# A fused transformer block: in its attention, the value product goes to the end of the next unit, and turned blocks go by DRAM

## The chip, the cores and the metric

The kernel is one program on one core of a Trainium2 chip. The time is the device time of one execution in microseconds; of the kernel before three executions were timed, and one more was profiled. TensorE is called PE, VectorE DVE, ScalarE ACT, GpSimd POOL and SyncE SP.

## The reference, cut to what matters

Four residual steps on x of shape (4, 512, 512). The change is in the third, an attention with 16 heads of width 128 whose keys and values come from `ctx_2048`.

```python
def _L1_xattn_ref(inputs_q, inputs_kv, Wq, Wk, Wv, Wo):
    q = (inputs_q @ Wq).reshape(b, sq, H, HD) * (1.0 / np.sqrt(HD))
    k = (inputs_kv @ Wk).reshape(b, skv, H, HD)
    v = (inputs_kv @ Wv).reshape(b, skv, H, HD)
    scores = jnp.einsum('bqhd,bkhd->bhqk', q, k)
    attn = jax.nn.softmax(scores, axis=-1)
    ctx = jnp.einsum('bhqk,bkhd->bqhd', attn, v).reshape(b, sq, H * HD)
    return ctx @ Wo

x = x + _L0_xattn_ref(_layernorm(x, axis=-1), ctx_2048, mask_Bx1xS2_ff0)
x = x + _L0_ffn_ref(_layernorm(x, axis=-1), ...)
x = x + _L1_xattn_ref(_layernorm(x, axis=-1), ctx_2048, L1_xattn_Wq, L1_xattn_Wk, L1_xattn_Wv, L1_xattn_Wo)
x = x + _L1_ffn_ref(_layernorm(x, axis=-1), L1_ffn_W1, L1_ffn_W2, L1_ffn_W3)
```

## The kernel before

Each step is a phase with a block of its own for each engine, and the engines meet at a barrier between phases. Every product of the attention is made from float32 numbers that are split into a high and a low part (`_hi`, `_lo`), in three matmuls: high by high, high by low, low by high (`three_pass`, line 46). ACT copies the high part out of the PSUM bank, DVE subtracts it from the bank to get the low part. POOL splits the weights and the turned probabilities, which lie in SBUF.

`attention_phase` (line 1109) works in 64 units. A unit is one head of one batch. Batches come in two pairs (`r`), a pair has 32 units in 8 groups (`g`) of four (`p` = 0 to 3): p = 0 and 2 are batch 0 of the pair, p = 1 and 3 batch 1, and each group covers two heads. The first and last group of a pair stand in the program by themselves, those between are a loop.

In unit n PE does: the scores of unit n (12 matmuls of 512 columns into four score banks), the queries of unit n+1 (12, into `qk_bank`), `weigh`, the product of the values with the turned probabilities of unit n-1 (12, into `vo_bank`), the keys of unit n+1 (12, again into `qk_bank`, so only when the low part of the queries is out), and the output projection of unit n-1 (12 matmuls in four tiles through two banks). Values of a whole group (four times 24 matmuls of 256 columns, `project_v`, also into `vo_bank`) stand between output tiles: two in p = 0, one in p = 1, one in p = 3.

The probabilities take the longest way. DVE takes the maxima (line 1417), ACT the exponentials (1330), DVE turns 32x32 blocks (1408) into `blocks`, then a reciprocal (1424) signals `p_movable`. SP then issues 16 transfers of 64 KB, SBUF to SBUF, that put the blocks in place (`move`, 1192 to 1197); they fill `pT_raw` in four quarters. For each quarter ACT makes the high part (`turned`, 1321) and POOL the low part (`low`, 1255), and only then `weigh` may run. ACT does its four quarters at the end of its unit.

Between the pairs lies the layer norm of batches 2 and 3. DVE takes its row statistics in one piece behind unit 1 (`stats.compute`, lines 94 to 126), and those of the last phase's batches 0 and 1 behind unit 33. In unit 31 PE turns the normalised rows through the score banks (`tensor_turn`, 187), ACT and DVE copy them out (195, 202).

Each engine works its own list in order; semaphores order the lists against each other. There is no scheduler: the order is that of the code.

## Time and profile before

| | |
|---|---|
| median of three runs | 2359.31 us (2358.37 to 2359.66) |
| the profiled execution | 2352.57 us, of which the span is 2350.9 us |
| attention, first scores to last output | 605 to 1790 us of the span |
| granted PE clock, mean of the span | 0.95 |
| PE busy over the span | 1977.7 us (84%) |

The profiled execution is one run; its own time is 6.7 us under the median. The span counts from the first to the last instruction. A row's "idle before" is the time in which its engine stood still ahead of it, with the work whose end released it. Matmuls are pipelined, so a row's duration (0.39 us) is longer than the distance to the next start; the distance is what a matmul costs.

### The profile page before, as it was taken

How to read it: one execution, taken by the hardware profiler on the slowest of the kernel's cores; microseconds unless marked ns; L12 is line 12 of the kernel's file. 1: busy time of each engine (PE TensorE's matmuls, PEld its weight loads, DVE VectorE, ACT ScalarE, POOL GpSimd, SP SyncE). 2: the span in 40 equal slices, each digit the busy share in tenths (PEclk: the TensorE clock that was granted, in tenths of full speed). 3: DMA queues.
4: the chain of work that ended last, by engine and by line, in shares of the span. 5: the costliest groups of instructions: out<-in, count | busy, mean ns of one | idle time of the engine just before them, and what ended most of it. 6: DMA issues, size and time to landing. Idle time of an engine off the chain costs nothing. (4 is left out here: it accounts for less than half of the span.)

```text
span 2350.9 us, 29076 instructions
## 1 busy us (share of the span) xinstructions
PE 1977.7 (84%) x9625; PEld 1618.6 (69%) x9625; DVE 1350.1 (57%) x2075; ACT 830.9 (35%) x1603; POOL 1047.1 (45%) x857
## 2 busy tenths in 40 slices
PE   0259858880879999999887999999996999999999
PEld 0127647660757787777776788787775788888887
DVE  7883558776565655656557566556565533333333
ACT  3212158770434444444433344444442211111111
POOL 2655532216555655656645665565645101222200
PEclk9779979995889999999988999999998999999999
DMA  4053399985223333333322332333322000000001
GB/s 163 0 211 99 122 321 383 381 300 166 81 71 95 85 87 92 85 96 92 103 73 76 91 96 77 92 100 83 85 70 90 25 12 28 27 27 27 0 1 72
DMA packets 138772, 245.90 MB, mean 105 GB/s; under 512 B 23872, under 2 KB 49216, under 8 KB 138688
## 3 DMA queue, kind: packets, MB, share of 16 engines
q1 hardware_dynamic: 121280, 186.11, 25.4%
q0 software_dynamic: 17408, 58.73, 8.7%
q8 instruction: 46, 0.75, 0.1%
q14 instruction: 38, 0.31, 0.0%
HBM read 136.22 MB, written 41.42 MB: 76 GB/s over the span
## 5 line engine op out<-in xcount | busy, mean ns | idle before, releaser
L1255 POOL TENSOR_TENSOR t_pT_lo<-t_pT_raw,t_pT_hi 128x512 fp32r<-128x512 f32 x256 | 329.1, 1291 | 380.7 <-ACT t_pT_hi L1321 374.5
L1321 ACT ACTIVATE t_pT_hi<-t_pT_raw 128x512 fp32r<-128x512 f32 x256 | 161.0, 630 | 296.5 <-DMA t_pT_raw<-t_blocks 296.4
L1408 DVE STREAM_TRANSPOSE t_blocks<-t_probs 128x512 f32<-128x512 f32 x256 | 172.0, 701 | 70.1 <-ACT t_probs L1330 68.9
L1714 DVE TENSOR_TENSOR f_lin<-f_lin,f_silu 128x512 f32<-128x512 f32 x64 | 44.6, 699 | 287.0 <-PE f_lin L51 287.0
L1330 ACT ACTIVATE t_probs<-t_score,t_sums 128x512 f32<-128x512 f32 x256 | 173.0, 681 | 87.1 <-DVE t_sums L1417 49.3
L1400 DVE SCALAR_TENSOR_TENSOR x_res<-t_out,t_sums,x_res 128x512 f32<-128x512 f32 x256 | 180.0, 743 | 10.3 <-PE t_out L51 10.3
L1641 POOL TENSOR_TENSOR f_w_hi<-w_raw,f_zeros 128x1024 fp32r<-128x1024 f32 x16 | 30.5, 1904 | 317.6 <-PE f_gate L51 314.3
L1417 DVE TENSOR_REDUCE t_sums<-t_score 128x1 f32<-128x512 f32 x256 | 162.4, 683 | 0.0
L51 PE MATMUL t_vo<-t_wv_hi,t_cT_hi 128*128 128x256 f32 x512 | 146.3, 286 | 1.8 <-DVE t_v_lo L1387 1.4
L1674 ACT ACTIVATE f_silu<-f_gate 128x512 f32<-128x512 f32 x64 | 38.3, 598 | 307.1 <-PE f_gate L51 307.1
L51 PE MATMUL t_vo<-t_wv_hi,t_cT_lo 128*128 128x256 f32 x512 | 144.8, 283 | 0.0
L51 PE MATMUL t_vo<-t_wv_lo,t_cT_hi 128*128 128x256 f32 x512 | 144.8, 283 | 0.0
L51 PE MATMUL t_qk<-t_cT_hi,t_wk_hi 128*128 128x512 f32 x256 | 105.2, 411 | 36.0 <-DVE t_q_lo L1378 35.8
L1383 DVE TENSOR_TENSOR t_k_lo<-t_qk,t_k_hi 128x512 fp32r<-128x512 f32 x64 | 44.2, 691 | 154.2 <-ACT t_k_hi L1304 154.2
L1387 DVE TENSOR_TENSOR t_v_lo<-t_vo,t_v_hi 128x512 fp32r<-128x512 f32 x64 | 44.2, 691 | 153.1 <-ACT t_v_hi L1310 153.1
L51 PE MATMUL t_vo<-t_pT_hi,t_v_hi 128*128 128x512 f32 x256 | 103.5, 404 | 29.0 <-POOL t_pT_lo L1255 29.0
L51 PE MATMUL t_qk<-t_xT_hi,t_wq_hi 128*128 128x512 f32 x256 | 101.7, 397 | 18.5 <-DVE t_xT_lo L202 18.5
L51 PE MATMUL t_out<-t_wo_hi,t_o_hi 128*128 128x512 f32 x256 | 102.0, 399 | 16.1 <-DVE x_res L1400 13.1
L1734 DVE TENSOR_TENSOR x_res<-f_down,x_res 128x512 f32<-128x512 f32 x128 | 87.9, 688 | 42.9 <-PE f_down L51 42.8
L51 PE MATMUL f_gate<-f_xT_hi,f_w_hi 128*128 128x512 f32 x256 | 101.0, 395 | 8.4 <-POOL f_w_lo L1644 5.3
L51 PEld LDWEIGHTS t_vo<-t_wv_hi,t_cT_hi 128*128 128x128 f32 x512 | 97.9, 191 | 10.3 <-DVE t_v_lo L1387 8.4
L51 PE MATMUL t_qk<-t_cT_lo,t_wk_hi 128*128 128x512 f32 x256 | 102.2, 399 | 0.0
...
## 6 DMA issues: line engine op xcount, KB each, us to landing
t_pT_raw<-t_blocks SPq DMA_DIRECT2D x1024, 64.0 KB, 2.0
e_up_raw<-in_L_ffn_Wrt_up_dram SPq DMA_DIRECT2D x47, 512.0 KB, 6.7
e_down_raw<-in_L_ffn_Wrt_down_dram SPq DMA_DIRECT2D x47, 512.0 KB, 6.3
...
e_xg<-tokens_by_expert SPq DMA_DIRECT2D x47, 256.0 KB, 6.5
outputs_by_expert<-e_y_out SPq DMA_DIRECT2D x47, 256.0 KB, 6.7
wq_raw<-in_L_xattn_Wq_dram POOLq DMA_DIRECT2D x32, 256.0 KB, 3.7
wk_raw<-in_L_xattn_Wk_dram POOLq DMA_DIRECT2D x32, 256.0 KB, 3.4
```

The costliest lines, as they stand in the source:

```text
L51: ins = pe.matmul(out, w(k), x(k), start=(k == 0 and j == 0), stop=(k == k_tiles - 1 and j == 2))
L1255: pool.tensor_tensor(pT_lo[:, q], pT_raw[:, q], f32(pT_hi[:, q]), ALU.subtract).then_inc(p_ready, 1)
L1321: act.activation(pT_hi[:, q], pT_raw[:, q], ACT.Copy).then_inc(p_hi_ready, 1)
L1330: act.activation(probs[:, t % 2, :], score_bank[t][:, :], ACT.Exp, bias=neg_max[:, t:t + 1], accum_out=total[:, t:t + 1]).then_inc(exp_rea ...
L1383: dve.tensor_tensor(k_lo[:, :], qk_bank[:, :], f32(k_hi[:, :]), ALU.subtract).then_inc(k_ready, 1)
L1387: dve.tensor_tensor(v_lo[:, b, 2 * half:2 * half + 2, :], vo_bank[:, :].rearrange("p (t d) -> p t d", t=2), f32(v_hi[:, b, 2 * half:2 * ha ...
L1400: dve.scalar_tensor_tensor(out=x_tile, in0=out_bank[t % 2][:, :], scalar=inv[:, b, t:t + 1], in1=x_tile, op0=ALU.mult, op1=ALU.add).then_i ...
L1408: dve.transpose(blocks[:, :, :, t, :].rearrange("p a t j -> p t a j"), probs[:, t % 2, :].rearrange("p (t a j) -> p t a j", a=Q4, j=BLK)). ...
L1417: dve.tensor_reduce(neg_max[:, t:t + 1], score_bank[t][:, :], AX.X, ALU.max, negate=True).then_inc(max_ready, 1)
L1674: act.activation(silu[:, k, :], gate_bank[k][:, :], ACT.Silu).then_inc(silu_ready, 1)
L1714: dve.tensor_tensor(lin_bank[k][:, :], lin_bank[k][:, :], silu[:, k, :], ALU.mult).then_inc(mid_done, 1)
L1734: dve.tensor_tensor(x_tile, down_bank[t][:, :], x_tile, ALU.add).then_inc(added, 1)
```

## The change

PE's order within a unit is new. Unit n now has: scores of n, queries of n+1, one piece of values (p = 0 to 2; it goes into score bank 1 once unit n's second exponential has read it), output tiles 0 and 1 of unit n-2, keys of n+1 (into score bank 0), output tiles 2 and 3 of n-2, and last `weigh` of unit n-1. In p = 3 the piece of values stands behind `weigh` and goes into score bank 3. Queries and head outputs have a bank of their own (`q_bank`, `o_bank`). The output of a unit is thus two units behind its scores, and four sums are kept instead of two.

On SP a unit issues 8 transfers of 256 KB: four from `blocks` to a DRAM buffer, each from 32 partitions, and four back from DRAM to 128 partitions of `pT_raw`. ACT handles the quarters of unit n-1 between the exponentials of unit n. DVE takes the row statistics in three pieces behind different units, and the layer norm's turning is spread over units 30 and 31.

```diff
-        sums = al.sb("sums", [4, TB])
-        neg_max, total, inv = sums[:, 0], sums[:, 1], sums[:, 2:4]
+        sums = al.sb("sums", [6, TB])
+        zeros, neg_max, inv = sums[:, 0], sums[:, 1], sums[:, 2:6]
-        qk_bank = al.ps("qk", [S])
-        vo_bank = al.ps("vo", [S])
+        q_bank = al.ps("q", [S])
+        o_bank = al.ps("o", [S])
...
-            def move(n):
-                sp.wait_ge(p_movable, n + 1)
+            def move(n, p):
                 for q in range(Q4):
-                    for a in range(Q4):
-                        dst = pT_raw[a * BLK:(a + 1) * BLK, q].rearrange("p t n -> p (t n)")
-                        src = blocks[q * BLK:(q + 1) * BLK, a].rearrange("p t u j -> p (t u j)")
-                        sp.dma_start(dst, src).then_inc(p_moved[q], 16)
+                    if q == 0:
+                        sp.wait_ge(p_movable, n + 1)
+                    elif not (known(n) and n == 0):
+                        sp.wait_ge(p_ready, (n - 1) * Q4 + (q + 1))
+                    sp.dma_start(moved[p % 2, q].rearrange("a i n -> i a n"),
+                                 blocks[q * BLK:(q + 1) * BLK].rearrange("p a t u j -> p a (t u j)")).then_inc(p_out[q], 16)
+                for q in range(Q4):
+                    sp.wait_ge(p_out[q], 16 * (n + 1))
+                    sp.dma_start(pT_raw[:, q].rearrange("p t n -> p (t n)"),
+                                 moved[p % 2, q].rearrange("a i n -> (a i) n")).then_inc(p_moved[q], 16)
...
             def group(r, g):
+                n, h1, h2 = 4 * g, 2 * g + 1, 2 * g + 2
+                boundary = known(g) and g == GROUPS - 1
+                final = known(g) and g == PAIRS * GROUPS - 1
+                if not (known(g) and g == 0):
+                    low(r, n - 1, after=("o", h1 - 2))
                 split(r, "q", h1, q_done, 2 * h1)
                 split(r, "k", h1, k_done, 2 * h1, after=("q", h1))
+                low(r, n, after=("k", h1))
+                split(r, "o", h1 - 1, out_done, 2 * TB * (h1 - 1))
+                low(r, n + 1, after=("o", h1 - 1))
+                if not final:
+                    split(r, "q", h2, q_done, 2 * h2)
+                    split(r, "k", h2, k_done, 2 * h2, after=("q", h2))
+                if boundary:
+                    ctx_lo(1, 0)
+                    ctx_lo(1, 1)
+                low(r, n + 2, after=None if final else ("k", h2))
+                if not final:
                     split(r, "v", g + 1, v_done, 4 * g + 4)
+                if boundary:
+                    ctx_lo(1, 2)
+                    ctx_lo(1, 3)
+                split(r, "o", h1, out_done, 2 * TB * h1, after=None if final else ("v", g + 1))
...
             def unit(r, g, p):
                 n = 4 * g + p
+                last = known(n) and n == LAST
+                if not (known(n) and n < 2):
+                    head_output(n - 2)
+                if p == 0:
+                    values(4 * g, 0, 0, score_bank[3])
                 for t in range(TB):
                     act.wait_ge(max_ready, n * TB + (t + 1))
+                    if not (known(n) and n == 0 and t < 2):
                         act.wait_ge(p_turned, n * TB + (t - 1))
                     act.activation(probs[:, t % 2, :], score_bank[t][:, :], ACT.Exp, bias=neg_max[:, t:t + 1],
+                                   accum_out=inv[:, p, t:t + 1]).then_inc(exp_ready, 1)
+                    if t == 3 and not last:
+                        query(n + 1)
+                    if not (known(n) and n == 0):
+                        turned(n - 1, t)
+                if p < 3:
+                    values(4 * g + 1 + p, (0, 1, 1)[p], (1, 0, 1)[p], score_bank[1])
                 if not last:
                     key(n + 1)
+                if known(n) and n in (UNITS - 2, UNITS - 1):
+                    i = n - (UNITS - 2)
+                    for c in (2 * i, 2 * i + 1):
+                        ctx_hi(1, c)
+                    ln.scalar_hi(act, 2 + i, xT_hi, i)
...
-                        dve.wait_ge(p_moved[q], 64 * n)
+                        dve.wait_ge(p_out[q], 16 * n)
...
             def unit(r, g, p):
                 n = 4 * g + p
+                last = known(n) and n == LAST
+                outputs = not (known(n) and n < 2)
+                before = r - 1 if p < 2 and known(g) and g == GROUPS else r
                 for t in range(TB):
                     dve.wait_ge(scored, n * TB + (t + 1))
                     dve.tensor_reduce(neg_max[:, t:t + 1], score_bank[t][:, :], AX.X, ALU.max,
                                       negate=True).then_inc(max_ready, 1)
+                    if p == 0 and t == 0:
+                        values(4 * g, 0, 0, score_bank[3])
+                turn(n, 0)
+                turn(n, 1)
+                if outputs:
+                    head_output(n - 2)
+                turn(n, 2)
+                turn(n, 3)
                 if not last:
                     project_q(n + 1)
+                dve.wait_ge(p_turned, (n + 1) * TB)
+                if not (known(n) and n == 0):
+                    dve.wait_ge(p_ready, (n - 1) * Q4 + 1)
+                dve.reciprocal(inv[:, p, :], inv[:, p, :]).then_inc(p_movable, 1)
+                if p < 3:
+                    values(4 * g + 1 + p, (0, 1, 1)[p], (1, 0, 1)[p], score_bank[1])
+                for t in range(2):
+                    if outputs:
+                        add(before, n - 2, (p - 2) % 4, t)
                 if not last:
                     project_k(n + 1)
                 for t in range(2, TB):
+                    if outputs:
+                        add(before, n - 2, (p - 2) % 4, t)
+                if known(n) and n in (UNITS - 2, UNITS - 1):
+                    i = n - (UNITS - 2)
+                    ln.vector_lo(dve, 2 + i, xT_hi, xT_lo, i)
+                    if i == 0:
+                        ln.vector_norm(dve, 3, 3)
 
             def group(r, g):
                 for p in range(4):
                     unit(r, g, p)
+                    if known(g) and g == 0:
+                        if p < 2:
+                            stats.read(dve, 2 + p)
+                        elif p == 2:
+                            stats.finish(dve, 2, 2)
+                        else:
+                            ln.vector_norm(dve, 2, 2)
+                    if known(g) and g == GROUPS:
+                        if 0 < p < 3:
+                            stats.read(dve, p - 1)
+                        elif p == 3:
+                            stats.finish(dve, 0, 2)
...
+                if not (known(n) and n == 0):
+                    pe.wait_ge(exp_ready, (n - 1) * TB + 1)
+                project("k", score_bank[0], b, cT_hi, cT_lo, k_done)
...
+                outputs = not (known(n) and n < 2)
+                if known(n) and n in (UNITS - 1, UNITS):
+                    pe.wait_ge(ln.lo_ready, (n - UNITS + 4) * TB)
                 pe.wait_ge(q_ready, n + 1)
                 pe.wait_ge(k_ready, n + 1)
                 for t in range(TB):
                     if not first:
                         pe.wait_ge(exp_ready, (n - 1) * TB + (t + 1))
+                        if t == 1:
+                            pe.wait_ge(v_ready, 4 * g + (0, 2, 3, 4)[p])
+                    if t == 3 and p == 0:
+                        pe.wait_ge(v_ready, 4 * g + 1)
                     three_pass(pe, score_bank[t][:, :], lambda k: q_hi[:, t * P:(t + 1) * P],
                                lambda k: q_lo[:, t * P:(t + 1) * P], lambda k: k_hi[:, :], lambda k: k_lo[:, :],
                                1).then_inc(scored, 1)
                 if not last:
                     project_q(n + 1, 1 - b, 2 * g + (p + 1) // 2 + 1)
+                if p < 3:
+                    project_v(n, (0, 1, 1)[p], (1, 0, 1)[p], 1)
+                if outputs:
+                    output(n - 2, b, 2 * g + p // 2, (0, 1))
+                if known(n) and n in (UNITS - 1, UNITS):
+                    pe.wait_ge(c_ready, 6 + 2 * (n - UNITS + 1))
                 if not last:
                     project_k(n + 1, 1 - b, 2 * g + (p + 1) // 2 + 1)
+                if outputs:
+                    output(n - 2, b, 2 * g + p // 2, (2, 3))
+                if known(n) and n in (UNITS - 2, UNITS - 1):
+                    pe.wait_ge(k_ready, n + 2)
+                    pe.wait_ge(v_ready, 4 * g + 4)
+                    ln.tensor_turn(pe, 2 + n - (UNITS - 2), bank_free=lambda t: pe.wait_ge(exp_ready, n * TB + (t + 1)))
                 if not first:
+                    weigh(n - 1, 1 - b, (1, 0, 0, 1)[p], 4 * g + (0, 2, 4, 4)[p])
+                if known(n) and n == UNITS - 1:
+                    pe.wait_ge(ln.lo_ready, 4 * TB)
+                if p == 3 and not last:
                     pe.wait_ge(w_ready["v"], g + 2)
+                    project_v(n, 0, 0, 3)
...
+            ln.tensor_turn(pe, 1, bank_free=lambda t: pe.wait_ge(ln.lo_ready, t + 1))
             pe.wait_ge(c_ready, 2)
+            pe.wait_ge(ln.lo_ready, TB + 1)
...
+            output(LAST - 1, 0, PAIRS * H, range(TB))
             weigh(LAST, 1, 1, 2 * PAIRS * H)
             output(LAST, 1, PAIRS * H, range(TB))
```

Of the lists of POOL, ACT, DVE and PE the diff shows the lines that stand there now; the old ones are in the kernel above. Bank names in the helpers are left out.

Three places in the lists of the engines. Semaphores that an earlier phase has freed show under that phase's name: `a_added` is here the semaphore of the maxima, `a_amax_ready` and `a_amax_over` those of queries and keys, `a_scale_ready` that of the values.

On ACT, unit 2 (p = 2), before:

```order
L1330 ACTIVATE t_probs,t_sums<-t_score,t_sums 128x512 [waits t_p_turned,a_added] x4
L1300 ACTIVATE t_q_hi<-t_qk 128x512 [waits a_amax_ready]
L1315 ACTIVATE t_o_hi<-t_vo 128x4x4x32 [waits t_o_done]
L1304 ACTIVATE t_k_hi<-t_qk 128x512 [waits a_amax_over]
L1321 ACTIVATE t_pT_hi<-t_pT_raw 128x512 [waits t_p_moved0]
L1321 ACTIVATE t_pT_hi<-t_pT_raw 128x512 [waits t_p_moved1]
L1321 ACTIVATE t_pT_hi<-t_pT_raw 128x512 [waits t_p_moved2]
L1321 ACTIVATE t_pT_hi<-t_pT_raw 128x512 [waits t_p_moved3]
```

And the same unit in the change:

```order
L1324 ACTIVATE t_o_hi<-t_o 128x4x4x32 [waits t_o_done]
L1343 ACTIVATE t_probs,t_sums<-t_score,t_sums 128x512 [waits t_p_turned,a_added]
L1330 ACTIVATE t_pT_hi<-t_pT_raw 128x512 [waits t_p_moved0]
L1343 ACTIVATE t_probs,t_sums<-t_score,t_sums 128x512 [waits t_p_turned,a_added]
L1330 ACTIVATE t_pT_hi<-t_pT_raw 128x512 [waits t_p_moved1]
L1343 ACTIVATE t_probs,t_sums<-t_score,t_sums 128x512 [waits t_p_turned,a_added]
L1330 ACTIVATE t_pT_hi<-t_pT_raw 128x512 [waits t_p_moved2]
L1343 ACTIVATE t_probs,t_sums<-t_score,t_sums 128x512 [waits t_p_turned,a_added]
L1311 ACTIVATE t_q_hi<-t_q 128x512 [waits a_amax_ready]
L1330 ACTIVATE t_pT_hi<-t_pT_raw 128x512 [waits t_p_moved3]
L1319 ACTIVATE t_v_hi<-t_score 128x512 [waits a_scale_ready]
L1315 ACTIVATE t_k_hi<-t_score 128x512 [waits a_amax_over]
```

The quarters (`t_pT_hi`) stood behind the unit's keys and belonged to the unit itself; now they stand between the exponentials and belong to the unit before, and each exponential but the first has one in front of it.

On SP, from the phase's first loads to the start of unit 1, before:

```order
L1189 DMA t_c_raw<-in_ctxT_dram 128x2x512 x2
L1189 DMA t_c_raw<-in_ctxT_dram 128x2x512 [waits a_c_in3] x2
L1197 DMA t_pT_raw<-t_blocks 32x512 [waits t_p_movable]
L1197 DMA t_pT_raw<-t_blocks 32x512 x15
L1197 DMA t_pT_raw<-t_blocks 32x512 [waits t_p_movable]
```

In the change, the blocks of unit 1, and the loads of the next pair's context that follow:

```order
L1197 DMA turned_blocks<-t_blocks 32x4x512 [waits t_p_movable]
L1197 DMA turned_blocks<-t_blocks 32x4x512 [waits t_p_ready] x3
L1201 DMA t_pT_raw<-turned_blocks 128x512 [waits t_p_out0]
L1201 DMA t_pT_raw<-turned_blocks 128x512 [waits t_p_out1]
L1201 DMA t_pT_raw<-turned_blocks 128x512 [waits t_p_out2]
L1201 DMA t_pT_raw<-turned_blocks 128x512 [waits t_p_out3]
L1189 DMA t_c_raw<-in_ctxT_dram 128x2x512 [waits a_c_in3] x2
```

Sixteen issues behind one wait became eight: the last three of the way out wait for POOL's low parts of the unit before (`t_p_ready`), and each transfer back waits until its quarter lies in DRAM.

On DVE, behind unit 1, before:

```order
L1383 TENSOR_TENSOR t_k_lo<-t_qk,t_k_hi 128x512
L1400 SCALAR_TENSOR_TENSOR x_res<-t_out,t_sums,x_res 128x512 x2
L1387 TENSOR_TENSOR t_v_lo<-t_vo,t_v_hi 128x512
L1400 SCALAR_TENSOR_TENSOR x_res<-t_out,t_sums,x_res 128x512 x2
L101 BN_STATS row_stats<-x_res 128x6 x8
L110 BN_AGGR mean_var<-row_stats 128x2 x8
L113 TENSOR_SCALAR mean_var<-mean_var 128x8
L114 TENSOR_SCALAR rstd_bits<-mean_var 128x8
L115 TENSOR_SCALAR rstd_root<-rstd_bits 128x8
```

In the change, from the second piece of statistics behind unit 1 to the start of the third piece behind unit 2:

```order
L101 BN_STATS row_stats<-x_res 128x6 x4
L1421 TENSOR_REDUCE t_sums<-t_score 128x1 x4
L1411 STREAM_TRANSPOSE t_blocks<-t_probs 128x4x4x32 x2
L1396 TENSOR_TENSOR t_o_lo<-t_o,t_o_hi 128x4x4x32
L1411 STREAM_TRANSPOSE t_blocks<-t_probs 128x4x4x32 x2
L1381 SCALAR_TENSOR_TENSOR t_q_lo<-t_q,t_q_hi 128x512
L1436 RECIPROCAL t_sums<-t_sums 128x4
L1390 TENSOR_TENSOR t_v_lo<-t_score,t_v_hi 128x512
L1403 SCALAR_TENSOR_TENSOR x_res<-t_out,t_sums,x_res 128x512 x2
L1386 TENSOR_TENSOR t_k_lo<-t_score,t_k_hi 128x512
L1403 SCALAR_TENSOR_TENSOR x_res<-t_out,t_sums,x_res 128x512 x2
L110 BN_AGGR mean_var<-row_stats 128x2 x8
```

All eight `BN_STATS` stood ahead of unit 2's maxima (`TENSOR_REDUCE`), and the chain behind `BN_AGGR` too. Now four and four stand behind units 0 and 1 and the chain behind unit 2; the head output's low part (`t_o_lo`) stands between the second and the third transposition.

## Rows read from the trace of the kernel before

**Rows 1.** Waits of PE from 605 to 1792: what waited, for what, total, times, longest.
```profile
PE t_qk L51 <- DVE t_q_lo L1378: 34.3, 20, 14.0
PE t_vo L51 <- POOL t_pT_lo L1255: 29.0, 16, 6.5
PE t_out L51 <- DVE x_res L1400: 13.1, 17, 0.8
```

**Rows 2.** Windows: stretch, length, busy PE, PEld, DVE, ACT, POOL; PEclk, DMA share, GB/s.
```profile
605.20:690.12 84.92, 65.74 (x314) 53.99 (x313) 52.29 (x97) 30.15 (x63) 39.53 (x35) 0.90 0.27 69
690.12:1112.92 422.80, 404.85 (x2018) 336.68 (x2016) 255.12 (x409) 179.53 (x384) 253.55 (x223) 1.00 0.35 90
1112.92:1203.52 90.60, 73.88 (x369) 62.40 (x368) 50.39 (x81) 38.64 (x78) 51.69 (x41) 0.91 0.35 96
1203.52:1286.08 82.56, 69.93 (x337) 58.01 (x336) 54.02 (x100) 29.11 (x63) 42.19 (x37) 0.92 0.28 74
1286.08:1706.21 420.13, 403.30 (x2018) 337.17 (x2016) 255.03 (x409) 179.62 (x384) 253.11 (x221) 1.00 0.34 89
1706.21:1791.28 85.07, 69.37 (x313) 55.27 (x311) 46.48 (x75) 30.30 (x64) 32.89 (x28) 0.94 0.23 56
```

**Rows 3.** Timeline of PE in unit 43: start, duration, operation, idle before.
```profile
1407.75 0.39 PE L51 MATMUL t_score<-t_k_hi,t_q_hi 128*128 128x512 f32 x1
...
1410.47 0.39 PE L51 MATMUL t_qk<-t_xT_hi,t_wq_hi 128*128 128x512 f32 x1
...
1414.80 0.50 PE L51 MATMUL t_vo<-t_pT_hi,t_v_hi 128*128 128x512 f32 x1 [1.45 <-POOL t_pT_lo L1255]
...
1422.47 0.28 PE L51 MATMUL t_vo<-t_wv_hi,t_cT_hi 128*128 128x256 f32 x1
...
1425.34 0.40 PE L51 MATMUL t_out<-t_wo_hi,t_o_hi 128*128 128x512 f32 x1
```

**Rows 4.** Timeline of DVE in unit 42, from the scores' maxima on.
```profile
1394.45 2.47 DVE L1417 TENSOR_REDUCE t_sums<-t_score 128x1 f32<-128x512 f32 x4
1396.88 1.31 DVE L1408 STREAM_TRANSPOSE t_blocks<-t_probs 128x512 f32<-128x512 f32 x2
...
1399.91 0.18 DVE L1424 RECIPROCAL t_sums<-t_sums 128x4 f32<-128x4 f32 x1
```

**Rows 5.** Timeline of ACT in unit 42.
```profile
1395.82 0.67 ACT L1330 ACTIVATE t_probs<-t_score,t_sums 128x512 f32<-128x512 f32 x1
...
1407.98 0.63 ACT L1321 ACTIVATE t_pT_hi<-t_pT_raw 128x512 fp32r<-128x512 f32 x1 [2.70 <-DMA t_pT_raw<-t_blocks]
```

**Rows 6.** The page's groups: POOL's low part of a quarter.
```profile
L1255 POOL TENSOR_TENSOR t_pT_lo<-t_pT_raw,t_pT_hi 128x512 fp32r<-128x512 f32 x256 | 329.1, 1291 | 380.7 <-ACT t_pT_hi L1321 374.5
```

**Rows 7.** The page: DMA issues, KB each, median us from issue to landing.
```profile
t_pT_raw<-t_blocks SPq DMA_DIRECT2D x1024, 64.0 KB, 2.0
...
e_xg<-tokens_by_expert SPq DMA_DIRECT2D x47, 256.0 KB, 6.5
outputs_by_expert<-e_y_out SPq DMA_DIRECT2D x47, 256.0 KB, 6.7
...
t_c_raw<-in_ctxT_dram SPq DMA_DIRECT2D x8, 512.0 KB, 3.9
```

**Rows 8.** Line 1197: issue times on SP, ns min/median/max.
```profile
L1197 SPq DMA_DIRECT2D t_pT_raw<-t_blocks x1024: 507/591/1973, 612.3 to 1775.6; - x171
```

**Rows 9.** Timeline of DVE between units 1 and 2: the row statistics.
```profile
643.42 4.96 DVE L101 BATCH_NORM_STATS2 row_stats<-x_res 128x6 f32<-128x512 f32 x8
648.42 0.64 DVE L110 BATCH_NORM_AGGREGATE mean_var<-row_stats 128x2 f32<-128x6 f32 x8
...
656.12 0.17 DVE L120 SCALAR_TENSOR_TENSOR rstd<-rstd_work,rstd_root 128x8 f32<-128x8 f32 x1
```

**Rows 10.** Timeline of PE behind the last unit's scores.
```profile
1779.64 0.79 PE L51 MATMUL t_vo<-t_pT_hi,t_v_hi 128*128 128x512 f32 x1 [6.52 <-POOL t_pT_lo L1255]
...
1786.08 0.50 PE L51 MATMUL t_out<-t_wo_hi,t_o_hi 128*128 128x512 f32 x1 [1.41 <-DVE t_o_lo L1393]
```

More of the change, by code:

```diff
@@ L1159, in attention_phase @@
         p_turned, p_movable = sem("p_turned"), sem("p_movable")
+        p_out = [sem(f"p_out{i}") for i in range(Q4)]
         p_moved = [sem(f"p_moved{i}") for i in range(Q4)]
@@ L1329, in unit @@
                         act.wait_ge(p_turned, n * TB + (t - 1))
                     act.activation(probs[:, t % 2, :], score_bank[t][:, :], ACT.Exp, bias=neg_max[:, t:t + 1],
-                                   accum_out=total[:, t:t + 1]).then_inc(exp_ready, 1)
-                boundary = known(n) and n == UNITS - 1
-                if boundary:
-                    for c in range(4):
-                        ctx_hi(1, c)
-                    ln.scalar_hi(act, 2, xT_hi, 0)
-                if not last:
-                    query(n + 1)
@@ L1367, in _ @@
             ctx_hi(0, 3)
+            ln.scalar_hi(act, 1, xT_hi, 1)
             key(0)
-            ln.scalar_hi(act, 1, xT_hi, 1)
-            values(0, 0, 0, None)
             run_groups(act, group)
+            head_output(LAST - 1)
+            for q in range(Q4):
+                turned(LAST, q)
             head_output(LAST)
@@ L1418, in unit @@
                                       negate=True).then_inc(max_ready, 1)
-                for t in range(TB):
-                    turn(n, t)
-                dve.wait_ge(p_turned, (n + 1) * TB)
-                if not first:
-                    dve.wait_ge(p_ready, n * Q4)
-                dve.reciprocal(inv[:, p % 2, :], total[:, :]).then_inc(p_movable, 1)
-                if boundary:
-                    ln.vector_lo(dve, 2, xT_hi, xT_lo, 0)
-                    ln.vector_norm(dve, 3, 3)
+                    if p == 0 and t == 0:
+                        values(4 * g, 0, 0, score_bank[3])
@@ L1434, in unit @@
+                dve.reciprocal(inv[:, p, :], inv[:, p, :]).then_inc(p_movable, 1)
[4 more added lines that the diff above has]
+                        add(before, n - 2, (p - 2) % 4, t)
                 if not last:
                     project_k(n + 1)
-                before = r - 1 if p == 0 and known(g) and g == GROUPS else r
-                for t in range(2):
-                    if not first:
-                        add(before, n - 1, 1 - p % 2, t)
@@ L1440, in unit @@
-                if p == 0:
-                    values(4 * g + 1, 0, 1)
-                elif p == 1:
-                    values(4 * g + 3, 1, 1)
-                elif p == 3 and not last:
-                    values(4 * g + 4, 0, 0)
-                for t in range(2, TB):
-                    if not first:
-                        add(before, n - 1, 1 - p % 2, t)
-                if p == 0:
-                    values(4 * g + 2, 1, 0)
+                for t in range(2, TB):
+                    if outputs:
+                        add(before, n - 2, (p - 2) % 4, t)
```

143 lines of the change are left out of this document (37 added, 106 removed).

## The prediction

> **What bounds the kernel now.** I read the busy shares by stage first, then who waits for whom on PE, then the timeline of single units. In the loops PE is busy for 404.85 of 422.80 us and 403.30 of 420.13 at a granted clock of 1.00, while DVE has 60%, ACT 42%, POOL 60% [rows 2]: PE sets the pace there, and only its own gaps can be won. In the four other stretches the clock is 0.90 to 0.94, a mix of full speed (2.4 GHz) with pieces at 1.2 GHz, and PE stands longer. The waits [rows 1] are of three kinds: for the low part of the queries (34.3 us, one of 14.0), for POOL's low parts of the turned probabilities (29.0 us, 16 waits, so about one per group, 6.5 at the very end), and for an output bank (13.1 us, 0.8 each).
>
> A clean unit gives PE's prices [rows 3]: 12 matmuls of 512 columns take 1410.47 - 1407.75 = 2.72 us, 24 of 256 columns 1425.34 - 1422.47 = 2.87. A group of four units has 20 blocks of the first kind and four of the second, 54.4 + 11.5 = 65.9 us. It takes 422.80/6 = 70.5 and 420.13/6 = 70.0. So a group holds about 4.3 us to be won, most of it in p = 3: the quarters of unit 42 come from SP at 0.59 us an issue, four issues a quarter [rows 8], the second quarter is copied at 1407.98 [rows 5], and the product that wants all four stands until 1414.80 with 1.45 us idle.
>
> **The change in a clean unit.** I write a timetable with T = 0 at the first score matmul of a unit with p = 1 or 2. PE: scores to 2.72, queries 5.44, values 8.31, output 9.67, keys 12.39, output 13.75, weigh 16.47. DVE's maxima run from 0.84 to 3.6 (four in 2.47 [rows 4]; each needs its scores). ACT: exponential 0 at 1.63, quarter 0 at 2.3, exponential 1 from 2.95 to 3.8, then quarter, exponential, quarter, exponential, queries, quarter 3 to 7.6, at 0.67 and 0.63 us each [rows 5]. DVE's transpositions at 3.6 and 4.2 (0.65 each in pairs [rows 4]), low part of the head output to 5.6, two more to 7.2, queries' low part 7.9, reciprocal 8.3. POOL's last low part of unit n-1: 7.6 + 1.29 [rows 6] = 8.9.
>
> What PE needs against this: values want exponential 1 (3.8) at 5.44, slack 1.6. Output wants the head's low part (5.6) at 8.31; but in p = 3 no values stand between, it is wanted at 5.44, and PE waits 0.25. Weigh wants 8.9 at 13.75 (11.1 in p = 3). The values' weights for p = 3's piece are split behind that, two passes over 1024 columns, at most four times 1.29 [rows 6]: 14.1, wanted at 13.9, so 0.2 late at worst; I take 0. In p = 0 the last score tile wants values' low part behind the first maximum, 0.2 late. So a group costs 65.9 + 0.45, plus 0.4 for what handovers leave open, an estimate: 66.8.
>
> **The way by DRAM.** It is off PE's path if quarter 0 of unit n lies in SBUF at T + 18.8, behind the next unit's exponential 0. `p_movable` is at 8.3, and the two transfers stand in a row, so each may take 5.2 us. The trace has no such pair. From below: 64 KB within SBUF land in 2.0 us, 512 KB from DRAM in rows of 2 KB in 3.9 [rows 7]; between them 256 KB lie near 2.7. From above: 6.5 and 6.7 us for 256 KB each way [rows 7], from the expert phase, where DMA is loaded; here the share is 0.34 [rows 2], and at most doubles to 0.68 with 1 MB each way per unit. I take 3 each: out 0 lands at 11.4, but SP also waits for POOL's last low part (8.9) before it issues out 3, so in 0 goes at 11.4, lands at 14.4, in 3 near 17. Cover of 4.4 us. SP's issues fall from 16 to 8 per unit, 9.4 to 4.7 us [rows 8], so the issue time pays for the way. Before unit n's quarter 0 can be copied, unit n's own exponential 0 must be through; a late quarter now stands in front of exponential 1 on ACT, and behind it wait the transposition, the output's low part, the queries and next unit's transfers.
>
> The Trainium skill (DMA: Bandwidth & Descriptors, "Anatomy of one DMA") speaks against a detour by DRAM: a fixed 2 us per transfer, most of it the write's receipt, with DRAM as the slowest target, plus bytes at 436 GB/s. By it a quarter takes about 2.6 us each way, an estimate from that page, and in 0 lands earlier than in my timetable. The trace agrees with the fixed part (2.0 us for 64 KB), though only for SBUF.
>
> **The special places.** Row statistics: 4.96 us for eight, a chain from 648.42 to 656.3, 7.9 us [rows 9]. Four statistics behind a unit (2.5 us) delay the next maximum by some 0.5 and stay within slack. The chain starts at 15.3 in the unit before, ends at T + 6.7: maxima come 5.9 late. In unit 3 (p = 3) and in unit 36 (p = 0) PE waits 6 us. After a wait of 6.52 us today, 12 matmuls and a wait of 1.41 take 1786.08 - 1779.64 = 6.44 [rows 10], 2.3 more than 2.72 + 1.41, since PE runs at 1.2 GHz there at first: 8 each in all.
>
> Stretch by stretch, profiled execution [rows 2]:
> - units 0 to 3, 84.92: unit 0 has no output and no weigh, 11.0 and 1.6 for the keys' low part; unit 1 13.7; unit 2 16.5; unit 3 24.5; with 2 for the cold start 68.3. Gain 16.6, which contains 5.4 us of weigh and output that move to the end.
> - units 4 to 27, 422.80: 6 x 66.8 = 400.8. Gain 22.0.
> - units 28 to 31, 90.60: two units 33.2; unit 30 with 16 transposes (at the 0.12 of a matmul of 256 columns, 1.9) 18.6; unit 31 with 1.9, 2.2 for the norm of four tiles that DVE puts ahead of its maxima (four times a transposition's 0.65 [rows 4], less slack), and 0.4: 21.0. Gain 17.8.
> - units 32 to 35, 82.56: 67.3. Gain 15.3.
> - units 36 to 59, 420.13: 400.8 + 8. Gain 11.3.
> - unit 60 to the next phase, 85.07: three units 49.7. In unit 63 weigh of 62 ends at 12.9, ACT copies the head, then the quarters from 13.7; POOL's four low parts take 5.2 and end at 19.5. Today weigh starts at 1779.64 and the next phase 11.6 us later [rows 10]; the same 11.6 give 31.1. Sum 80.8, gain 4.3.
> - ahead of unit 0 the turning stands before the keys, a loss of 0.6.
>
> Sum 86.7 us: 2352.6 - 86.7 = 2265.9 for the profiled execution; the median of the runs is 6.7 above it, so 2359.3 - 86.7 = 2272.6.
>
> **The rivals.**
> - *The round trip is late.* If a quarter takes more than 5.2 us each way, exponential 1 is late in all units. At 6.6 us, near the upper rows [rows 7], it is 2.8 late: 1.2 per unit with p < 3, and 3.0 in p = 3 instead of 0.25, where the output's low part hangs on it, 6.3 a group, 101 us over 16. That gives 2373, slower. For it: the load nearly doubles, and a unit's transfers queue together. Against: 4.4 us of cover, and a share of 0.34 now. The Trainium skill (same page, "Latency and other measured facts") has DRAM access at 0.2 us and at 2 us under high load; that would be this rival's way, and no stretch of the attention here shows it.
> - *PE's new waits cost each a little.* Today's wait for an output bank costs 0.8 us, 17 times [rows 1]. Values and keys now take banks that ACT has just left. With 0.8 in each unit, 51 us: 2324. Against: by the timetable these banks are free 1.6 us and more ahead.
> - *The chain of statistics costs what it did.* If the 7.9 us ahead of the maxima are not hidden, and units 30 and 31 keep half of their wait, 26 to 30 us come back: 2300.
>
> **Chances.** The forecast 0.60 with its own range 2260 to 2294 (unknown landing within cover, each small wait 0 to 1 us a group more), the chain 0.12, small waits 0.13, the late round trip 0.10, something unnamed that eats the gain 0.05. A difference under 0.2% (4.7 us) is not told from none. Faster 0.87, same 0.03, slower 0.10. The range that leaves out 2 in 10 is 2256 to 2328: it takes in the chain, the small waits up to their price, and stops short of the late trip.
>
> **What would show it.** Right: loops of 66 to 68 us a group, PE's wait for `t_pT_lo` gone except at the end, transfers to and from the DRAM buffer landing in 2.5 to 4 us, ACT's wait for `t_pT_raw` near zero, PE waiting 6 us in units 3 and 36 for work behind the maxima. Wrong: if ACT waits for the transfers in every unit, or transfers land beyond 5 us, the round trip is the bound and the time above 2330; if PE shows a wait of about 0.8 us at each value or key block, the banks are.

## The result and the profile after

The changed kernel takes 2254.16 us (median of four runs, 2248.89 to 2258.36) against 2358.84 us of the kernel before (2357.57 to 2359.66): a ratio of 0.9556, 95% interval 0.9534 to 0.9577. It is faster by 104.7 us. My sum gave 2272.6, with a range from 2256: the sign and most of the terms are right, the time lies 18.4 us under the forecast and 1.8 us below the range. Its profiled execution took 2255.5 us (span 2253.9).

First the windows of the kernel after, over the same units as [rows 2] (length, busy PE, PEld, DVE, ACT, POOL; PEclk, DMA share, GB/s):

```profile
613.22:674.54 61.32, 58.75 (x302) 49.56 (x301) 46.64 (x93) 27.74 (x60) 36.62 (x32) 1.00 0.61 173
674.54:1074.04 399.50, 398.88 (x2018) 338.38 (x2017) 250.69 (x409) 174.12 (x384) 252.96 (x222) 1.00 0.56 158
1074.04:1146.82 72.78, 70.54 (x370) 59.65 (x369) 50.18 (x80) 36.71 (x76) 49.64 (x39) 1.00 0.57 159
1146.82:1213.36 66.54, 66.44 (x338) 56.40 (x337) 49.87 (x91) 29.00 (x64) 44.15 (x40) 1.00 0.57 159
1213.36:1613.73 400.37, 398.80 (x2019) 338.38 (x2017) 251.75 (x417) 174.23 (x384) 252.47 (x221) 1.00 0.55 157
1613.73:1694.80 81.07, 69.56 (x327) 55.74 (x325) 48.47 (x78) 31.07 (x67) 35.85 (x31) 0.98 0.40 111
```

In the loops PE is busy for 398.88 of 399.50 us, so a group of 66.6 us holds practically no gap. The clock is now 1.00 in the stretches at either end of a loop too, where [rows 2] have 0.90 to 0.92; the longest stand of PE in these is now 2.0 us, where it was 14.0.

Three of PE's waits over the attention (total, times, longest):

```profile
PE t_out L51 <- DVE t_o_lo L1396: 7.1, 4, 2.6
...
PE t_o L51 <- POOL t_pT_lo L1260: 3.0, 1, 3.0
...
PE t_out L51 <- DVE x_res L1403: 1.2, 3, 0.9
```

The page's rows on the route, KB and median us from issue to landing:

```profile
turned_blocks<-t_blocks SPq DMA_DIRECT2D x256, 256.0 KB, 3.8
t_pT_raw<-turned_blocks SPq DMA_DIRECT2D x256, 256.0 KB, 4.1
```

The 34.3 us for the queries' low part are gone, and of the 29.0 for POOL [rows 1] only the 3.0 behind the last unit's scores are left. The 7.1 us for the head's low part are four waits: 1.1 in unit 3, 2.0 in unit 31, 2.6 and 1.4 from unit 63 on. ACT's wait for the turned tile is 2.6 us in all. The timeline of PE in unit 43, which answers to [rows 3]:

```profile
1330.78 0.39 PE L51 MATMUL t_score<-t_k_hi,t_q_hi 128*128 128x512 f32 x1
...
1341.87 0.39 PE L51 MATMUL t_o<-t_pT_hi,t_v_hi 128*128 128x512 f32 x1
...
1344.59 0.28 PE L51 MATMUL t_score<-t_wv_hi,t_cT_hi 128*128 128x256 f32 x1
```

POOL's in the same unit:

```profile
1335.65 3.82 POOL L1260 TENSOR_TENSOR t_pT_lo<-t_pT_raw,t_pT_hi 128x512 fp32r<-128x512 f32 x3
1339.42 1.89 POOL L1238 TENSOR_TENSOR t_wv_hi<-wv_raw,t_sums 128x1024 fp32r<-128x1024 f32 x1
1341.39 2.40 POOL L1242 TENSOR_TENSOR t_wv_lo<-wv_raw,t_wv_hi 128x1024 fp32r<-128x1024 f32 x1
```

The value product starts at T + 11.1, as the timetable had it for p = 3; POOL's last low part is done at T + 8.7 (8.9). The values' weights are split at 1343.8, 0.8 us ahead of their product.

**The ledger**, profiled execution against profiled execution, gain in us:

| stretch | forecast | measured |
|---|---|---|
| units 0 to 3 | 16.6 | 23.6 |
| units 4 to 27 | 22.0 | 23.3 |
| units 28 to 31 | 17.8 | 17.8 |
| units 32 to 35 | 15.3 | 16.0 |
| units 36 to 59 | 11.3 | 19.8 |
| unit 60 to the next phase | 4.3 | 4.0 |
| first norm of the attention to unit 0 | -0.6 | -5.7 |
| all phases outside the attention | 0 | -1.8 |
| sum | 86.7 | 97.1 |

The remaining 7.6 between 97.1 and 104.7 is no mechanism: the profiled execution of before was 6.3 us below its median, that of after 1.3 us above.

### The profile page after: what moved, and what is told of

The parts are those of the page before. It is cut to its first block and busy times, and to the rows that moved or that the text cites. A ratio compares the mean times of both kernels' runs of the same rounds, so it can differ in the third digit from the quotient of the medians.

```text
span 2253.9 us, 28904 instructions
## 1 busy us (share of the span) xinstructions
PE 1957.6 (87%) x9625; PEld 1614.8 (72%) x9625; DVE 1340.8 (59%) x2075; ACT 816.9 (36%) x1603; POOL 1047.9 (46%) x857
## 5 line engine op out<-in xcount | busy, mean ns | idle before, releaser
L1655 POOL TENSOR_TENSOR f_w_hi<-w_raw,f_zeros 128x1024 fp32r<-128x1024 f32 x16 | 30.4, 1902 | 317.7 <-PE f_gate L51 313.9
L51 PE MATMUL t_score<-t_wv_hi,t_cT_lo 128*128 128x256 f32 x512 | 144.9, 283 | 0.0
L51 PE MATMUL t_score<-t_wv_lo,t_cT_hi 128*128 128x256 f32 x512 | 144.9, 283 | 0.0
L51 PE MATMUL t_score<-t_wv_hi,t_cT_hi 128*128 128x256 f32 x512 | 144.5, 282 | 0.0
L1386 DVE TENSOR_TENSOR t_k_lo<-t_score,t_k_hi 128x512 fp32r<-128x512 f32 x64 | 44.3, 692 | 128.4 <-ACT t_k_hi L1315 128.4
L1324 ACT ACTIVATE t_o_hi<-t_o 128x512 fp32r<-128x512 f32 x64 | 38.3, 598 | 223.4 <-PE t_o L51 223.4
L1315 ACT ACTIVATE t_k_hi<-t_score 128x512 fp32r<-128x512 f32 x64 | 38.3, 598 | 209.9 <-PE t_score L51 209.9
L51 PE MATMUL t_q<-t_xT_hi,t_wq_hi 128*128 128x512 f32 x256 | 100.7, 393 | 4.6 <-DVE t_xT_lo L202 4.6
L51 PE MATMUL t_score<-t_k_hi,t_q_hi 128*128 128x512 f32 x256 | 101.2, 395 | 4.0 <-issue 1.5
L51 PE MATMUL t_o<-t_pT_hi,t_v_hi 128*128 128x512 f32 x256 | 100.4, 392 | 3.0 <-POOL t_pT_lo L1260 3.0
L51 PE MATMUL t_score<-t_cT_hi,t_wk_hi 128*128 128x512 f32 x256 | 100.8, 394 | 0.1
```

The source lines that it names most:

```text
L51: ins = pe.matmul(out, w(k), x(k), start=(k == 0 and j == 0), stop=(k == k_tiles - 1 and j == 2))
L1315: act.activation(k_hi[:, :], score_bank[0][:, :], ACT.Copy).then_inc(k_hi_ready, 1)
L1324: act.activation(o_hi[:, :].rearrange("p (u q j) -> p q u j", q=Q4, j=BLK), o_bank[:, :].rearrange("p (q u j) -> p q u j", q=Q4, j=BLK), A ...
L1386: dve.tensor_tensor(k_lo[:, :], score_bank[0][:, :], f32(k_hi[:, :]), ALU.subtract).then_inc(k_ready, 1)
```

## The experiments

Each series ran beside fresh runs of the kernel before; "base" is the changed kernel, unchanged. The edits are shown in shortened form. The length of a unit or stretch is from the one profile of its run.

**1. The base again (twice).**

> The changed kernel once more, unchanged, as the base of the other runs of this chip. Its four runs so far spread from 2248.9 to 2258.4 us, against 2357.6 to 2359.7 of the kernel before. If the spread belongs to the kernel, the runs of this one again differ by 5 to 10 us, with a median of 2250 to 2258; if one odd run made it, they lie within 2 us.

2263.21 us (2261.04 to 2265.98) where before took 2366.61: ratio 0.9554 (0.9541 to 0.9567). The second, on another chip:

> The changed kernel once more, as the base of the other runs of this chip: 0.9555 of the kernel before, as in the two earlier series, with 5 to 10 us between its runs.

2260.14 (2254.57 to 2269.16) against 2368.68: 0.9544 (0.9523 to 0.9564). The ratio holds, the level does not: the same kernel of before is 8 to 10 us slower on these chips and there spreads by 7 to 12 us too. So the spread is not the change's alone. Attention's first norm starts anywhere from 580 to 595 us in the profiles, with the same code ahead of it. Below I compare ratios, or stretches inside one profile.

**2. Statistics in one piece.** Behind unit 1 (and 33), as the kernel before had them:

```
-  if p < 2: stats.read(dve, 2 + p)
-  elif p == 2: stats.finish(dve, 2, 2)
-  else: ln.vector_norm(dve, 2, 2)
+  if p == 1: stats.compute(dve, 2, 2); ln.vector_norm(dve, 2, 2)
```

> The row statistics, their chain and (in the first stretch) the norm stand in one piece behind units 1 and 33, the rest is the changed kernel. Theory (the split into pieces is what shrank my term for units 3 and 36): DVE then puts 4.96 us of statistics, 3.7 to 7.9 us of chain and 2.2 to 3 us of norm ahead of the maxima of unit 2, so these come 9 to 13 us late against 1.6 us of slack, and 7 to 11 us late in unit 34; together 13 to 22 us more with the lower clock behind each wait, less the 2.5 us that units 3 and 36 now lose: 2265 to 2274 us. Rival (a unit of the new order has slack enough that the pieces did not matter): within 3 us of the changed kernel.

2276.56 us, 13.4 above the base on this chip (ratios 0.9612 and 0.9554). Unit 2 takes 25.46 us instead of 16.50, unit 34 22.77 instead of 16.50, and units 3 and 36 get 1.3 and 1.0 back: 12.9. The theory holds, at the lower end of its 13 to 22 us, since even here the chain took 3.7 us (POOL idle). In this profile unit 31 took 22.46 us too, but the edit does not touch it: with the same stand of PE of 2.0 us, unit 31 takes 20.8 to 20.9 us at a clock of 1.00 in six profiles and 22.5 at 0.92 in three.

**3. POOL kept busy beside the chain.**

```
+  if known(g) and g == 0:          # POOL, behind the key weights of unit 2
+      for i in range(3): pool.tensor_tensor(xn[i + 1], xn[0], xn[0], ALU.add)
```

> Three additional additions of 128x512 on POOL (1.0 to 1.3 us each, into a buffer that nothing reads then) behind its key weights of unit 2, where DVE runs the chain of row statistics and POOL stood idle. Theory (two operations of the chain, the scalar one and the one with two tensors, are held up while POOL works): the chain takes 6.5 to 8 us as in the kernel before instead of 3.7, single links 0.9 to 2.2 us instead of 0.17, PE waits 3 to 5 us in unit 3 and the time rises by 3 to 7 us. Rival (the chain was slow before for another reason, or the links do not depend on POOL): chain 3.7 us, every link 0.17, time within 1 us.

DVE and POOL in that run, behind unit 2:

```profile
660.89 3.04 POOL L1281 TENSOR_TENSOR t_ln_xn<-t_ln_xn 128x512 f32<-128x512 f32 x3
661.20 2.76 DVE L113 TENSOR_SCALAR mean_var<-mean_var 128x8 f32<-128x8 f32 x1
664.00 0.17 DVE L114 TENSOR_SCALAR rstd_bits<-mean_var 128x8 uint32<-128x8 uint32 x1
```

One link, of eight elements a row, takes 2.76 us instead of 0.17 and ends with POOL's third addition; the rest run at 0.17. The chain takes 6.3 us (expected 6.5 to 8), PE's wait for the head's low part rises from 1.1 to 3.7, unit 3 from 17.92 to 23.11 us. Half of these 5.2 us is the wait, the other half goes with the clock, 0.85 in unit 3 instead of 1.00. Timed, 2267.41 us, 4.2 above the base; the single runs overlap (2261.6 to 2270.6 and 2261.0 to 2266.0), so it is the trace that shows it, not the time.

**4. The norm in another form of DVE.**

```
-  dve.tensor_scalar(xn, x, mean, rstd, ALU.subtract, ALU.mult)
+  dve.scalar_tensor_tensor(out=xn, in0=x, scalar=mean, in1=rstd broadcast to 512, subtract, mult)
```

> The norm of a tile is written as scalar_tensor_tensor (x minus mean, times the row's factor as a broadcast second tensor) in place of tensor_scalar with two scalars; same values. Theory (the form decides who is held up by POOL: in the trace scalar_tensor_tensor never shows it): the four tiles of the norm of batch 1 ahead of unit 0 take 2.8 us instead of 12.7, PE reaches unit 0 about 5 us earlier, the start of the last phase gains some too: 2240 to 2250 us. Rival (the Trainium skill, SBUF - State Buffer, 'two separate sides': an operation of DVE with two inputs in SBUF contends with POOL for the shared ports as the scalar form in its fast mode does): the four tiles still take 8 us and more, the time is within 2 us of the changed kernel, or up to 2 us longer since the new form takes 0.7 us instead of 0.54 where POOL is idle.

```profile
600.79 13.51 DVE L171 SCALAR_TENSOR_TENSOR t_ln_xn<-x_res,mean_var,rstd 128x512 f32<-128x512 f32 x4
```

13.5 us instead of 12.6, and 2269.94 us, 6.7 above the base, 2.4 of it in unit 31 (23.29 for 20.87). My theory fell: this form is held up as well. I had read its absence from the slow links as immunity; it had only stood behind others that had already waited for POOL, and in the chains ahead of the attention (four elements a row) it shows means of 0.44 and 0.61 us in the base's profile. What the Trainium skill says (SBUF — State Buffer, "SBUF: two separate sides": a DVE operation in a two-port mode, or with two inputs in SBUF while POOL reads SBUF, and an operation of POOL shut each other out of a shared pair of ports for a whole instruction) fits the trace here. Low parts and maxima, which read PSUM and at most one SBUF tensor, stay at 0.65 to 0.74 us beside POOL. The page speaks of one instruction; in run 3 the link waited until the third of three was through.

**5. The norms on ACT.** First only batch 1, ahead of unit 0; then batch 3, behind unit 30, too.

```
+  act.activation(xn[j], x[i], ACT.Identity, bias=shift[i], scale=rstd[i])   # shift = -mean * rstd, one DVE link
-  ln.vector_norm(dve, 1, 1)      # and, in the second kernel, ln.vector_norm(dve, 3, 3)
```

> The norm of batch 1 ahead of unit 0 is done by ACT (x times the row's factor plus a shift, 4 activations of about 0.6 us behind its copies of batch 0) and no longer by DVE beside POOL; the shift is one small operation of DVE. Theory (DVE's 12.6 us for four tiles beside POOL are what PE waits for ahead of unit 0): ACT is done 2.5 us behind its copies, PE's three waits of 1.5 to 1.8 us between the turnings go, unit 0 starts 4 to 6 us earlier, and the time falls by as much. Rival (the prologue is bound by POOL's splits of the values' weights and the context, which end at the same time): the waits move to another releaser, within 1 us of the changed kernel.

> As the last one, and the norm behind unit 30 by ACT too, so DVE's maxima of unit 31 don't stand behind 3.9 us of it. Theory: the first exponential of unit 31 comes about 3 us earlier, unit 31 takes 17.5 to 18.5 us instead of 20.9, the time is another 2 to 3.5 us lower. Rival: ACT's 2.4 us ahead of the head's output cost the same: no difference from the last one.

With batch 1 alone: 2260.19 us, the base's 2260.14. The way from the first norm to unit 0 is 25.2 us, against 30.4 in the base's profile, yet the median did not move. The profiles offer a reason: DVE's norm of batch 1 takes either 12.2 to 12.7 us (6 of the 8 profiles whose prologue is the changed kernel's, 30.1 to 30.8 us long) or 6.7 to 7.7 (the other two, 24.4 and 25.2, in which POOL had a break of 0.8 to 1.6 us ahead of the context's third tile). I take it that ACT's norm removes the long case and gains nothing on the short one. That is not shown: how often each falls outside the profiles, and what decides it, stays open. With both norms: 2255.89 us, ratio 0.9537 (0.9516 to 0.9558), unit 31 18.70 us instead of 20.86, just above the 17.5 to 18.5 expected.

> The version with the norms of batches 1 and 3 on ACT once more, on another chip: 0.9537 of the kernel before in the first series, whose interval of 0.9516 to 0.9558 holds the changed kernel's 0.9544 to 0.9556 too. If its 2 us in unit 31 and a prologue of 25 us instead of 25 to 31 are real, the ratio is again 0.952 to 0.954; if it is no faster than the changed kernel, 0.955 to 0.956.

2255.18 us, 0.9527 (0.9514 to 0.9540). The base has 0.9544 to 0.9556 in three series, this version 0.9537 and 0.9527. That would be some 4 us faster, but the intervals overlap and the base did not run beside the second series; shown are the 2.2 us of unit 31 (18.67 in this profile too).

**6. The old route in the new order.** 16 transfers of 64 KB within SBUF per unit, no DRAM.

> The new order with the old route: 16 transfers of 64 KB within SBUF per unit, straight from the blocks to the turned tile, no DRAM; all else is the changed kernel. In my timetable the reciprocal is at T + 8.3, 16 issues of 0.59 us end at T + 17.7, quarter 0 lands near T + 12.5 (needed T + 18.8) and quarter 3 near T + 20, needed about T + 23.5. Theory A (the gain is the order's, the route by DRAM is worth nothing here): within 4 us of the changed kernel. Rival B (the route is what makes the order possible, since SP's 9.4 us of issues and the waits for POOL between them make quarters 2 and 3 late): 0.5 us and more a unit, 2285 us or above, with ACT waiting for the turned tile.

2264.77 us, ratio 0.9580 (0.9555 to 0.9604), some 6 us above the base's ratio, with intervals that overlap. Units 4 to 27 take 399.52 us, the route by DRAM 399.50. It loses 5.2 us in the short first units: units 2 and 3 take 18.98 and 20.29 us, where DVE's transpositions wait 5.1 us for the blocks to be read out. Another 2.3 are lost from unit 63 on. Theory A holds for the loops; what the route is worth, it is worth at the two ends.

**7. The new route in the old order.**

```
-  sp.dma_start(dst, src).then_inc(p_moved[q], 16)      # 4 per quarter, within SBUF
+  sp.dma_start(moved[p % 2, q], blocks[q]); ... sp.dma_start(pT_raw[:, q], moved[p % 2, q])
```

> The kernel before with only the route changed: per unit 4 transfers out to DRAM and 4 back instead of 16 within SBUF; order, banks and waits as before. Theory A (the route alone is worth nothing, since the second issue of a quarter waits for the landing of the first): quarters land 7.9 to 10 us behind the reciprocal as before, time 2350 to 2368 us. Rival B (SP's issue time was the limit of the kernel before, so 8 issues instead of 16 make the last quarter 3 us earlier in each unit): 2320 to 2340 us.

2382.03 us, 1.0088 of the kernel before (1.0068 to 1.0109): slower by 20, worse than either theory. ACT's copies of the quarters of unit 42 (p = 2), first and last of the kernel before:

```profile
1404.65 0.62 ACT L1321 ACTIVATE t_pT_hi<-t_pT_raw 128x512 fp32r<-128x512 f32 x1
...
1412.78 0.63 ACT L1321 ACTIVATE t_pT_hi<-t_pT_raw 128x512 fp32r<-128x512 f32 x1 [1.87 <-DMA t_pT_raw<-t_blocks]
```

All four of this run:

```profile
1433.21 1.31 ACT L1324 ACTIVATE t_pT_hi<-t_pT_raw 128x512 fp32r<-128x512 f32 x2 [4.45 <-DMA t_pT_raw<-turned_blocks]
1434.90 0.63 ACT L1324 ACTIVATE t_pT_hi<-t_pT_raw 128x512 fp32r<-128x512 f32 x1 [0.38 <-DMA t_pT_raw<-turned_blocks]
1435.82 0.63 ACT L1324 ACTIVATE t_pT_hi<-t_pT_raw 128x512 fp32r<-128x512 f32 x1 [0.29 <-DMA t_pT_raw<-turned_blocks]
```

The reciprocal was at 1424.05, so the first copy comes 9.2 us behind it, against 4.7 before (1404.65, behind 1399.91 [rows 4]). The last comes no later (11.8 against 12.9), but all four come within 2.6 us, and POOL's four low parts then stand in a row until 1439.49, 15.4 us behind the reciprocal instead of 14.8. PE's waits from the first scores on:

```profile
PE t_vo L51 <- POOL t_pT_lo L1258: 29.7, 14, 3.2
...
PE t_vo L51 <- DVE t_v_lo L1390: 13.8, 14, 2.6
```

In eleven of the loops' twelve units with p = 3 PE stands 2.0 to 3.2 us for POOL, where it stood 1.4 to 2.0, and in six of them the granted clock is 0.92, where it was 1.00. The wait for the values' low part was 1.4 us, once, before; what makes it late stays open. Without the order, 8 issues buy nothing.

**8. A third leg.** Each quarter is copied once more from DRAM to DRAM.

> The changed kernel with a third leg: each quarter is copied once more from DRAM to DRAM before it is read back, so 12 transfers a unit in three legs. A leg takes 4 us in the trace, so quarter 0 lands near T + 20.5 instead of T + 16.4, quarter 3 near T + 24. Theory (the round trip has cover up to T + 18.8, as in the prediction; beyond it each unit loses what the quarters are late): 1.5 to 3 us late at exponential 1, of which 0 to 1.4 reach PE where values stand between and more where p = 3; 30 to 110 us in all, 2285 to 2365 us. Rival (cover is larger, ACT's place for the quarters is not what PE waits for): within 10 us of the changed kernel.

2299.40 us, ratio 0.9729 (0.9704 to 0.9753), 41 us above the base's ratio. ACT's waits:

```profile
ACT t_pT_hi L1334 <- DMA t_pT_raw<-turned_blocks: 106.6, 61, 3.9
```

ACT waits 61 times, 1.75 us each; of it 2.4 to 3.0 us a group reach PE (414.09 and 418.14 us for six groups, against 399.50 and 400.37). The third leg lands in 4.4 us. By issue and landing in the two traces, quarter 0 lands at T + 14.7 to 16.3 in the changed kernel's loops, where ACT does not wait, and at T + 20.0 to 24.0 here, where it does; the timetable's cover ends at T + 18.8, between the two. Units with p = 0 and 1 lose 0.5 us, those with p = 2 nothing, those with p = 3 1.5 to 1.9. So the prediction's late round trip is a real mechanism, and falls hardest on p = 3 as it had it; its 6.3 us a group was for 2.8 us of delay.

**9. The value product in mid-unit**, ahead of the next keys. In units 30 and 31 it stays at the end, and ACT's copy of a head also waits for output tiles; all else is as after.

> The value product stands ahead of the next keys, in the middle of the unit, instead of at its end; banks, route and the output's lag as in the changed kernel. Theory (the end of the unit is what hides POOL's low parts): in units with p = 3 it is wanted at T + 6.8 and POOL is done at T + 8.9, in p = 1 and 2 wanted at 9.7, in p = 0 at 9.7 too, so PE waits about 2.1 us for POOL once a group and 0 to 0.5 elsewhere: 34 to 60 us over the 16 groups with the value's low parts, 2288 to 2314 us where the changed kernel has 2254, ratio to the changed kernel 1.015 to 1.027. Rival (the gain comes from the output's lag and the banks, not from the place of the product): within 5 us.

```profile
PE t_o L51 <- POOL t_pT_lo L1260: 22.8, 16, 1.7
```

2326.83 us, ratio 0.9829 (0.9808 to 0.9849): 66.7 above the base, beyond my 34 to 60. A group takes 70.1 us, 3.5 more. The wait for POOL comes once a group as expected (1.4 on average, 1.7 at most, computed 2.1). The rest I had not seen: the keys now end 1.4 us ahead of the next scores, their copy and low part take 1.3 and the handovers, and the units with p = 0 to 2 lose 0.3 to 0.7 each. In the changed kernel the value product covers those too. The 70.1 us are what a group took in the kernel before (70.5 and 70.0): in the loops the banks and the output's lag gain nothing without the product's place, and the 42 us that this version still gains lie in the stretches around them.

## Why the prediction was off

- **Loops, right.** A group was to cost 66.8 and costs 66.6; the places of PE and POOL in the timetable hold to 0.3 us. The reciprocal comes at T + 7.5 to 7.9, not 8.3.
- **Route, right, with wrong sizes.** A leg takes 3.8 to 4.1 us where I took 3 (each might take 5.2): still in cover. The 2.6 us that I had worked out from the Trainium skill (DMA: Bandwidth & Descriptors, "Anatomy of one DMA") lie below both; its fit is for transfers that POOL issues, and SP issues these. Run 6 shows that the order, not the route, wins the loops, run 8 that beyond the cover PE loses.
- **Units 28 to 31 and the end, right** to 0.3 us (unit 30 18.55 for 18.6, unit 31 20.85 for 21.0). Unit 31 has luck in it: DVE's norm took 3.9 us where I took 2.6, and the clock stayed at 1.00, as it did not in three other profiles.
- **The chain in units 3 and 36, the term that failed.** "In unit 3 (p = 3) and in unit 36 (p = 0) PE waits 6 us", 8 each with the clock. Measured: 1.1 us of wait in each, unit 3 1.2 us longer than an ordinary unit with p = 3 (17.86 for 16.68), unit 36 1.0 longer than one with p = 0, clock 1.00:

```profile
663.38 0.50 PE L51 MATMUL t_out<-t_wo_hi,t_o_hi 128*128 128x512 f32 x1 [1.10 <-DVE t_o_lo L1396]
...
1216.65 0.47 PE L51 MATMUL t_score<-t_k_hi,t_q_hi 128*128 128x512 f32 x1 [1.06 <-DVE t_v_lo L1390]
```

That is 13.8 of the 17.2 us by which the attention's units gained more than forecast; 2 more are the "cold start" of unit 0 that never came. Against them stands a slip: the terms of units 0 to 3 add up to 69.3, not 68.3, so the gain was put 1.0 too high, and the forecast by its own terms is 2273.6. I had taken the 7.9 us of [rows 9] for the chain's own length, and they were not: between its shown rows, three links of the kernel before stood for POOL.

DVE's timeline of the kernel before, the rows that [rows 9] leave out:

```profile
649.10 2.18 DVE L113 TENSOR_SCALAR mean_var<-mean_var 128x8 f32<-128x8 f32 x1
...
651.52 0.97 DVE L115 TENSOR_SCALAR rstd_root<-rstd_bits 128x8 uint32<-128x8 uint32 x1
...
652.72 1.56 DVE L119 TENSOR_TENSOR rstd_work<-rstd_work,mean_var 128x8 f32<-128x8 f32 x1
```

POOL in the same stretch; each of the three links ends within 0.05 us of one of its operations:

```profile
648.88 2.37 POOL L1237 TENSOR_TENSOR t_wv_lo<-wv_raw,t_wv_hi 128x1024 fp32r<-128x1024 f32 x1
651.42 1.04 POOL L1233 TENSOR_TENSOR t_wq_hi<-wq_raw,t_zeros 128x512 fp32r<-128x512 f32 x1 [0.17 <-POOL t_wv_lo L1237]
...
652.97 1.27 POOL L1237 TENSOR_TENSOR t_wq_lo<-wq_raw,t_wq_hi 128x512 fp32r<-128x512 f32 x1
```

The same links in the kernel after, behind unit 2:

```profile
655.35 0.63 DVE L110 BATCH_NORM_AGGREGATE mean_var<-row_stats 128x2 f32<-128x6 f32 x8
656.02 0.17 DVE L113 TENSOR_SCALAR mean_var<-mean_var 128x8 f32<-128x8 f32 x1
...
656.43 0.17 DVE L115 TENSOR_SCALAR rstd_root<-rstd_bits 128x8 uint32<-128x8 uint32 x1
...
656.84 0.17 DVE L119 TENSOR_TENSOR rstd_work<-rstd_work,mean_var 128x8 f32<-128x8 f32 x1
```

2.18 + 0.97 + 1.56 is 4.2 us above three times 0.17, just the difference between 7.9 and 3.7. Run 3 shows the cause by bringing it back, and that the rest of the term was of the right scale: with a chain of 6.3 us unit 3 takes 23.11 us, 6.4 more than an ordinary one. Behind unit 35 POOL does hold two links (0.90 and 1.58), the chain takes 5.8 us, and unit 36 still loses only 1.0: DVE is done with a unit of p = 3 at T + 12.3, not at the 15.3 that I took from the others, so the chain ends at T + 1.6 and not at T + 6.7. There the starting place was wrong by more than the length.

- **The prologue, a term of the wrong size.** I took 0.6 for turning ahead of the keys. In the profiled execution it was 5.7: the norm of batch 1, 12.65 us beside POOL, now stands in front of PE's turning instead of behind the keys. The place alone does not cost it: in the kernel before this norm took 6.2 us, and in the profiles of runs 3 and 9, where it took 6.7 and 7.7, the way to unit 0 is 25.2 and 24.4 us, as before the change (25.1). The 0.6 left out that POOL can double the norm. DVE's row:

```profile
591.31 12.65 DVE L171 TENSOR_SCALAR t_ln_xn<-x_res,mean_var,rstd 128x512 f32<-128x512 f32 x4
```

PE's turning, which waits for each of its tiles:

```profile
601.13 1.12 PE L187 MATMUL t_score<-ident,t_ln_xn 128*128 128x128 f32 x4 [1.93 <-DVE t_ln_xn L171]
...
604.02 1.12 PE L187 MATMUL t_score<-ident,t_ln_xn 128*128 128x128 f32 x4 [1.77 <-DVE t_ln_xn L171]
```

- **The base.** I added the gain to the median of before, 6.7 us above its profiled execution. That distance was the one execution's own, and after stands 1.3 on the other side: with both, 7.6 of the 18.4 us of the miss. The terms make 10.4, the rest is that the median of before moved by 0.5.
- **The range.** Its lower end lay 17 under the forecast, with no case worked out in which a feared cost is absent; its upper end was 55 above.
